# Attention on one Trainium2 core: both inverses in other units, and the high half of the maxima rows on ScalarE

## The reference

```python
x = L0_attn_x
xn = _layernorm(x, axis=-1)
x = x + _L0_attn_ref(xn, W_qkv, W_o) + _L0_ffn_ref(xn, w_fc, w_proj)

def _L0_attn_ref(x, W_qkv, W_o):           # 16 heads of 32
    qkv = jnp.einsum('bld,ed->ble', x, W_qkv).reshape(b, 3, H, L, D_H)
    Q, K, V = (qkv[:, 0], qkv[:, 1], qkv[:, 2])
    scores = jnp.einsum('bhqd,bhkd->bhqk', Q, K) * D_H ** (-0.5)
    attn = jax.nn.softmax(scores, axis=-1)
    out = jnp.einsum('bhqk,bhkd->bhqd', attn, V)
    out = out.transpose(0, 2, 1, 3).reshape(b, L, D_IN)
    return jnp.einsum('bld,ed->ble', out, W_o)
```

## Time and profile before

| | |
|---|---|
| median of 3 executions | 3328.11 us (3327.81 to 3333.6) |
| profiled execution | 3329.19 us, of which 3327.4 us are its span from first to last instruction |
| PE busy | 3225.1 us, 97% |
| DVE busy | 2450.7 us, 74% |
| ACT busy | 1982.9 us, 60% |
| POOL busy | 1831.4 us, 55% |
| granted TensorE clock, mean | 0.981 |

### The profile page before, as it was taken

How to read it: one execution, slowest core, us unless ns; L and a number is a source line. 1 busy time by engine, 2 the same in 40 slices (tenths; PEclk the granted TensorE clock), 3 DMA queues, 4 the chain that set the end, 5 groups by cost and what they waited for, 6 DMA issues and landing times.

```text
span 3327.4 us, 73253 instructions
## 1 busy us (share of the span) xinstructions
PE 3225.1 (97%) x30336; PEld 1541.1 (46%) x30336; DVE 2450.7 (74%) x3456; ACT 1982.9 (60%) x2955; POOL 1831.4 (55%) x658
## 2 busy tenths in 40 slices
PE   3899999999999999998999999999999999999899
PEld 2344444444444444443444444444444444444344
DVE  7666666666676666666888888888888888888644
ACT  4444444444444444441688888888888888888711
POOL 0322323222333332220689889888988988988800
PEclk7899999999999999997899999999999999999999
DMA  4122222223132322224334443433433343343296
GB/s 159 75 87 78 92 91 80 88 83 81 79 81 102 83 85 85 90 68 99 60 77 82 81 81 70 89 76 75 84 80 83 70 89 74 72 87 64 72 336 233
DMA packets 376062, 309.34 MB, mean 93 GB/s; under 512 B 300672, under 2 KB 317056, under 8 KB 365440
## 3 DMA queue, kind: packets, MB, share of 16 engines
q1 hardware_dynamic: 375744, 304.69, 34.4%
HBM read 96.99 MB, written 139.46 MB: 71 GB/s over the span
## 4 chain that ended last, share of the span: by engine, by line
PE 49%; issue 1%; DVE 1%; POOL 1%; ACT 1%; DMA 1%; SPq 0%; POOLq 0%; ACTq 0%; DVEq 0%
PE es_for_maxima_and_scores L1088 26%; PE outputs L1109 13%; PE misc L1143 6%; PE es_for_maxima_and_scores L1184 3%; DVE half_maxima L1019 1%; POOL probs_sum L935 1%; ACT probs L967 0%; DMA k_stackT<-attention_scratch 0%; PE misc L1126 0%; DMA q_stackT<-stack_scratch 0%; POOL out_normed L942 0%; DVE q_stackT L1042 0%; ACT k_stackT L978 0%; ACT k_stackT L973 0%; DMA q_stackT<-maxima_rows 0%
## 5 line engine op out<-in xcount | busy, mean ns | idle before, releaser
L1019 DVE TENSOR_REDUCE half_maxima<-es_for_maxima_and_scores 128x1 f32<-128x512 f32 x2048 | 1275.5, 682 | 249.1 <-PE es_for_maxima_and_scores L1088 233.7
L967 ACT ACTIVATE probs<-es_for_maxima_and_scores,scalars 128x512 f32<-128x512 f32 x2048 | 1247.9, 696 | 316.5 <-PE es_for_maxima_and_scores L1088 313.1
L935 POOL TENSOR_TENSOR probs_sum<-probs_sum,probs 128x2048 f32<-128x2048 f32 x224 | 1026.5, 4583 | 23.2
L1088 PE MATMUL es_for_maxima_and_scores<-k_stackT,q_stackT 96*32 96x512 f16 x8192 | 851.4, 389 | 12.1 <-DMA q_stackT<-stack_scratch 11.2
L1088 PE MATMUL es_for_maxima_and_scores<-q_stackT,k_stackT 98*32 98x512 f16 x8192 | 839.5, 383 | 10.5 <-issue 7.2
L1109 PE MATMUL outputs<-probs,v_rows 128*32 128x512 f32 x4096 | 538.9, 594 | 2.3 <-ACT probs L967 0.8
L403 POOL TENSOR_TENSOR gelu_sum<-gelu_sum,gelu_out 128x1024 f32<-128x1024 f32 x96 | 254.9, 2655 | 451.5 <-ACT gelu_out L578 451.5
L1088 PEld LDWEIGHTS es_for_maxima_and_scores<-q_stackT,k_stackT 98*32 98x32 f16 x8192 | 326.6, 137 | 350.7 <-ACT probs L967 112.4
L935 POOL TENSOR_TENSOR probs_sum<-probs 128x2048 f32<-128x2048 f32 x64 | 293.2, 4581 | 226.3 <-ACT probs L967 226.3
L1088 PEld LDWEIGHTS es_for_maxima_and_scores<-k_stackT,q_stackT 96*32 96x32 f16 x8192 | 244.9, 96 | 314.3 <-DVE half_maxima L1019 172.7
L641 PE MATMUL psA<-x_hi,ternary_fcT 128*128 128x512 f16 x1024 | 388.1, 379 | 1.9 <-DVE x_lo L449 1.4
(11 more groups left out here) (135 smaller groups left out, 3300.6 us busy)
## 6 DMA issues: line engine op xcount, KB each, us to landing
stack_scratch<-hi_hi_lo_hi_rows SPq DMA_DIRECT2D x32, 1536.0 KB, 5.1
stack_scratch<-hi_hi_lo_hi_rows SPq DMA_DIRECT2D x32, 576.0 KB, 5.9
v_scratch<-v_rows_out SPq DMA_DIRECT2D x32, 576.0 KB, 6.9
x_rows<-in_L_attn_x SPq DMA_DIRECT2D x16, 1024.0 KB, 4.9
x_plus_ffn_scratch<-x_rows SPq DMA_DIRECT2D x16, 1024.0 KB, 3.9
v_rows<-v_scratch SPq DMA_DIRECT2D x32, 512.0 KB, 4.5
inverse_denominators<-denominators_scratch SPq DMA_DIRECT2D x256, 64.0 KB, 2.0
attention_scratch<-out_normed SPq DMA_DIRECT2D x64, 256.0 KB, 2.1
```

The lines of the kernel that those rows point to most:

```text
L935: nc.gpsimd.tensor_tensor(acc[:, hf], pr[:, 0] if j == 1 else acc[:, hf], pr[:, j], ALU.add).then_inc(added, 1)
L967: nc.scalar.activation(pr[:, w % 8, h, :], psS[:, bank(g, HG * w + h), :], ACT.Exp, scale=keep["scal"]["escale"]).then_inc(exp_done, 1)
L1019: nc.vector.tensor_reduce(mx[:, slot(n, 2), h, t, kh:kh + 1], psX[:, bank(n, r), :], axis=AX.X, op=ALU.max).then_inc(max_done, 1)
L1088: last = nc.tensor.matmul(out[q:q + 32, :], stationary[:, q:q + 32], moving, start=start, stop=stop)
```

## The change

The tables move the steps behind a denominator. The inverse of a group's first half goes from unit 15 of the same group to unit 2 of the next, that of the second half from unit 7 of the next group to unit 10. Spreading goes with them; normalising goes from units 2 and 9 to 4 and 12, storing from units 3 and 10 to 6 and 15. For the last group, the inverse and the spreading of its first half, which have no next group to stand in, come behind the loop on DVE and SP.

The high half of the maxima rows is made by ACT, between the third and the fourth exponential of unit 14 (for the first group, where there are no exponentials yet, alone). DVE makes the low half as before, but behind its third maximum of unit 14 instead of its second.

```diff
-INVERT = {7: (1, 1), 15: (0, 0)}
-SPREAD = {7: (1, 1), 15: (0, 0)}
-NORMALISE = {2: (1, 0), 9: (1, 1)}
-STORE = {3: (1, 0), 10: (1, 1)}
+INVERT = {10: (1, 1), 2: (1, 0)}
+SPREAD = {10: (1, 1), 2: (1, 0)}
+NORMALISE = {4: (1, 0), 12: (1, 1)}
+STORE = {6: (1, 0), 15: (1, 1)}
...
             groups(sp, body)
+            spread(GROUPS - 1, 0)
             load_out_tile(2)
...
+            def split_rows(n):
+                act.wait_ge(a_full, lin(n, 1, 1))
+                wait(act, aug_loaded, lin(n, 32))
+                nc.scalar.activation(rows[:, 0, :], psM[0:HG * KT_N, 0:P], ACT.Copy, scale=1.0 / AUG_UNIT).then_inc(high_rows, 1)
...
             def body(g, units):
-                if not exists(g):
-                    return
                 for w in units:
+                    if not exists(g):
+                        if w == ROWS_AT and exists(shift(g, 1)):
+                            split_rows(shift(g, 1))
+                        continue
                     for h in range(HG):
                         exp(g, w, h)
+                        if h == 2 and w == ROWS_AT and exists(shift(g, 1)):
+                            split_rows(shift(g, 1))
...
-            def split_rows(n):
+            def low_rows(n):
+                wait(dve, aug_loaded, lin(n, 32))
                 dve.wait_ge(a_full, lin(n, 1, 1))
-                wait(dve, aug_loaded, lin(n, 32))
-                nc.vector.tensor_scalar(rows[:, 0, :], psM[0:HG * KT_N, 0:P], 1.0 / AUG_UNIT, None, ALU.mult).then_inc(high_rows, 1)
                 dve.wait_ge(high_rows, lin(n, 1, 1))
                 nc.vector.scalar_tensor_tensor(rows[:, 1, :], psM[0:HG * KT_N, 0:P], 1.0 / AUG_UNIT, rows[:, 0, :],
                                                ALU.mult, ALU.subtract).then_inc(rows_ready, 1)
...
-                        if k == 1 and w == ROWS_AT and exists(shift(g, 1)):
-                            split_rows(shift(g, 1))
+                        if k == 2 and w == ROWS_AT and exists(shift(g, 1)):
+                            low_rows(shift(g, 1))
 
             nc.vector.memset(ones[:], AUG_UNIT).then_inc(ones_set, 1)
             groups(dve, body)
+            invert(GROUPS - 1, 0)
```

## The result

The changed kernel takes 3355.93 us (median of 4 executions, 3353.43 to 3357.1); the kernel before took 3329.49 us (4 executions) beside it. The ratio is 1.0077, with a 95% interval of 1.0059 to 1.0094: slower by 26.4 us, where +21.1 was predicted. The time lies 6.7 us above the forecast of 3349.2, near the upper end of its range (3336 to 3357). The profiled execution after took 3357.1 us (span 3355.3; before: span 3327.4).

A forecast was written before the change was run, and what follows sets the result against it. PE's order of work was taken as the bound, busy 48.51 of a group's 48.56 us. Terms 0 + 0 + 19.2 - 2.5 + 4.4 = +21.1 us on the median of 3328.11 gave 3349.2 us, range 3336 to 3357.

The forecast's parts named there:

- Inverses: DVE, units 7 and 15 to 10 and 2: gain between 0 and 15 us, taken as 0, hidden in DVE's idle time.
- High half on ACT: Unit 14, before ACT's fourth exponential: one added instruction of 0.3 us, hidden in 0.46 us of idle time, cost 0.
- Low half behind the third maximum: DVE, unit 14: rows issued 0.96 us late, 0.34 slack, PE 0.62 late in 31 groups, +19.2 us (14 to 23).
- Late landings: Groups whose row DMA already lands late pay the whole 0.96 us; no separate term in the sum.
- Next to last group: SP's queue, unit 10: 1 MB projection loads, and the last group's rows behind them, earlier, -2.5 us (0 to -4).
- The end: SP's queue, last group: store waiting for POOL delays projection tile 2's load by 5.7, then tile 3, +4.4 us (0 to 6).
- A: Rival: DVE was the pace, so 0.76 us less work there per group gives 3306 us; chance 0.05.
- B: Rival: the rows' lateness is hidden by 1 us of slack from landing to matmul, only the ends remain, 3330 us; chance 0.07.
- C: Rival: ACT's output copy in unit 8 waits for POOL's later normalisation; at 1.3 us delay 3365 us; chance 0.04.
- D: Rival: each late group start drops PE's clock to 1.2 GHz, 56 us on top, 3405 us; chance 0.02.

The follow-up runs named there:

- e2: Kernel before with only the moved inverses, spreading, normalising and storing; both halves of the maxima rows stay on DVE at the old place: 3332.01 us, ratio 1.0010.
- e1: Changed kernel with the low half back behind DVE's second maximum of unit 14, the high half still on ACT: 3339.69 us, ratio 1.0040.
- e4: Kernel before with only the low half moved behind DVE's third maximum; the high half stays on DVE, nothing on ACT: 3355.12 us, ratio 1.0082.
- e3: Kernel before with the rows' change alone: high half on ACT, low half on DVE behind the third maximum, old tables: 3356.33 us, ratio 1.0086.
- e5: Kernel before with two further copies of the high half's size on DVE ahead of the high half, into an unread tile: 3346.83 us, ratio 1.0054.
- e7: Changed kernel with the last store of group 30 moved behind the loads of projection tile 2 in SP's queue: 3348.78 us, ratio 1.0059.
- e6: Kernel before with the four 1 MB projection loads of group 30 issued in unit 2 instead of unit 10: 3321.65 us, ratio 0.9978.
- e12: Kernel before with early loads, rows transposed in unit 13, ACT's copies moved, the change's tables, and last store behind tile 2's loads: 3343.14 us, ratio 1.0036.

## Why the prediction was right, step by step

*Inverses, 0.* Right: e2's group is the old one, and units 7, 10 and 11 show it in the chain of waits.

*High half on ACT, 0.3 us, hidden.* Right in the changed kernel: 0.25 us, in the gap ahead of the fourth exponential, which shrinks from 0.46 to 0.37. The Trainium skill (VectorE: DVE Perf Modes, the section on the TRN2 errata) gave an estimate of 0.25 for it, and the trace agrees. In the place of e1, where DVE waits for it, it makes the low half 0.34 late, and the slack covers nearly all of it.

*Low half behind the third maximum, +19.2.* Right in mechanism and size. Its parts against the trace: the third maximum starts 0.44 behind its matmuls (0.45 predicted), the low half 0.61 behind that (0.60), it ends 0.96 later (0.96), the slack is 0.33 (0.34), and 0.63 is lost in a group (0.62). Measured 18.9 in 30 groups; the first group loses 0.24 of its own, not 0.62. From landing to first matmul the median of the groups falls from 0.42 us to 0.09, which is the slack by another way, 0.33. e4 has the loss without ACT, e1 has ACT without most of the loss.

*Late landings.* The prediction let groups with a late landing pay 0.96, within its bounds and outside the sum. With the slack gone there are also more of them that count: PE's waiting for them rises from 3.0 to 5.3 us, and to 7.6 to 9.2 in e1, e3, e4 and e5. This term was missing, +2.3; each of these figures is of one execution. So was another, +1.7: the steps of a group are 0.05 to 0.07 us longer in the kernels with later rows (after, e1, e3, e4, e7; 0.03 in e5); why stays open.

*Next to last group, -2.5.* Right in mechanism (e2: -2.0, e6), mis-sized in the changed kernel: -0.7. The windows view says why (columns as in the earlier trace rows; 4 us behind PE's starts of two groups that waited):

```profile
2979.20:2983.20 4.00, 4.00 (x64) 2.42 (x68) 2.84 (x5) 3.18 (x6) 0.67 (x1) 1.00 0.54 143
3079.07:3083.07 4.00, 4.00 (x40) 2.00 (x44) 1.64 (x3) 1.84 (x3) 0.87 (x1) 0.63 0.17 66
```

Group 30 itself starts late and in part at half clock (40 matmuls in the 4 us, where group 28 has 64), it takes until the transpose 45.94 us instead of 44.28, which makes the inverse in unit 10, and so the loads, later by as much: 1.7 us of the gain are gone. The bound that I put up to 0 covers it.

*The end, +4.4.* The size is right (+4.1), the path only in part: I had tile 2's lateness pass through ACT and SP to tile 3. In relation to the last group's start the load of tile 2 was 6.3 us later (5.7 predicted), and tile 3's input 4.4 (4.7 by the terms of the prediction). But PE already waits at tile 2 itself, 2.71 us, and runs in part at half clock behind it, for another 1.7; tile 3's input then stood ready (3212.97) ahead of PE (3213.68). I had checked the slack of tile 3 and not that of tile 2. The loss does not hang on the half clock, as e1 shows, whose queue at the end is the same (timeline of PE, tiles 2 and 3):

```profile
3181.48 0.39 PE L1194 MATMUL es_for_maxima_and_scores<-woT_hi,k_stackT 128*128 128x512 f16 x1 [2.97 <-DVE q_stackT L1051]
...
3192.94 0.39 PE L1194 MATMUL es_for_maxima_and_scores<-woT_hi,k_stackT 128*128 128x512 f16 x1 [0.93 <-DVE q_stackT L1051]
```

There the clock stays at 1.00 behind tile 2, PE waits for tile 3 as predicted, and starts it 80.71 us behind the last group's start; in the changed kernel it is 80.72. The two paths end at the same time, and e1's end is no shorter (222.92 against 222.34). e7 shows that the store is the cause of both.

So the three predicted terms came to 18.9 - 0.7 + 4.1 = 22.3 us instead of 21.1. The rest of the 27.9 is late landings, longer steps and the first group's start, none of which was in the sum.

*The rivals.* A is refuted by e2, B by the windows of a group. C did not come in the changed kernel, but its mechanism is real (e12). D came in single places, group 30 and tile 2, not at each late start: the window of a whole group has clock 1.00, and group 28, above, starts at the full clock behind a longer wait. What the Trainium skill says of kernels that pay for the clock at each wait (TensorE: Matmul & The Clock Gate, on HAM oscillation) does not apply to waits of 0.44 us, as PE has ahead of each group here: the trace shows 1.00 with them.

## What to carry to other kernels

Moving an instruction to an idle engine is worth nothing while another engine's order is the bound, and it costs when the instruction that depends on it ends up behind a wait in its own engine's order: look for the chain with the least slack (here 0.34 us from landing to matmul) and for what each edit does to its first link. Margins that are measured in tenths of a microsecond should be given away nowhere, since they also absorb the occasional late DMA; making the rows at the end of the unit before, and clearing SP's queue ahead of them, gave 0.37% without taking work from any engine. Two edits that are each free (moved tables, moved copies) can meet in one buffer, so the waits of the combined kernel have to be read anew.

## What the runs showed of the hardware

*Late landings come with fetched instructions.* The rows' second DMA lands 1.84 to 1.88 us behind its issue in most groups, and up to 3.9 in a few. The DMA view of the changed kernel, from issue to PE's start, of the group that starts at 2187.83 (on time) and of group 30 (late); both hold the same 96 packets of the rows:

```profile
q1 hardware_dynamic: 96, 0.02, 3.0%
issues: line engine op xcount, KB each, median us to landing
q_stackT<-maxima_rows SPq DMA_DIRECT2D x2, 8.0 KB, 1.8
```

```profile
q1 hardware_dynamic: 96, 0.02, 2.4%
q8 instruction: 1, 0.02, 2.1%
issues: line engine op xcount, KB each, median us to landing
q_stackT<-maxima_rows SPq DMA_DIRECT2D x2, 8.0 KB, 2.7
```

One 16 KB packet of instructions travels in the late flight. I call a group's pair of row DMAs late when one of the two lands more than 1.9 us behind its issue, and give it a packet (queue 8 or 14) when one starts between 0.4 us ahead of the first issue and 2.4 us behind it. In the traces of before and after, groups 1 to 30, all 15 late pairs have a packet, and so have 5 of the 45 others. In all 14 traces 117 of the 157 pairs with a packet are late, and 2 of the 263 without one. So not each packet makes a landing late. That the packet is the cause is argued from this, and was not tried: no run moved a fetch.

*The clock falls behind some waits and not behind others of the same length.* PE's starts of groups 28 and 30 in the changed kernel, from the timeline:

```profile
2979.20 0.44 PE L1098 MATMUL es_for_maxima_and_scores<-q_stackT,k_stackT 98*32 98x512 f16 x4 [1.89 <-issue]
```

```profile
3079.07 0.44 PE L1098 MATMUL es_for_maxima_and_scores<-q_stackT,k_stackT 98*32 98x512 f16 x4 [1.75 <-issue]
```

The longer wait left the granted clock at 1.00 (2.4 GHz). Behind the shorter one it was 0.63 over the 4 us above, a part of them at 1.2 GHz, where sets of four matmuls start 0.43 us apart (3082.39 and 3082.82) instead of 0.22 (3083.59 and 3083.81); that cost 1.7 us. e4 has one such fall at a group's start, e7's profiled execution three, and e1, e3 and e5 have none behind waits of 1.0 to 1.8 us. What tells them apart the traces don't show.
